# Value products of two key steps issued together, in an attention and LoRA-router kernel on one core

## The reference, cut to what matters

```python
# x: (2, 2048, 1024); wq, wo: (1024, 1024); wk, wv: (1024, 32); 32 heads of 32, one shared key/value head
h = layernorm(x)
q = (h @ wq).reshape(B, T, 32, 32); k = h @ wk; v = h @ wv
scores = einsum('bqhd,bkd->bhqk', q, k) / sqrt(32)      # causal
probs  = softmax(scores)
out    = einsum('bhqk,bkd->bqhd', probs, v) @ wo
x = x + layernorm(out)
h = layernorm(x)
router = 8 * softmax(h @ Wr.T + br)                      # 8 experts
low    = einsum('bsd,hrd->bshr', h, A)                   # rank 16 each
x = x + layernorm(2 * einsum('bshr,hor,bsh->bso', low, B, router))
```

## Time and profile before

| what | value |
|---|---|
| median of three runs | 3582.85 us |
| the profiled execution: its time, its span | 3581.36 us, 3579.6 us |
| TensorE busy | 3306.6 us, 92% |
| VectorE busy | 2299.5 us, 64% |
| GpSimd busy | 2121.2 us, 59% |
| ScalarE busy | 1567.7 us, 44% |
| mean granted TensorE clock | 0.966 |

### The profile page before, as it was taken

How to read it: one execution, slowest core, us unless ns; L and a number is a source line. 1 busy time by engine, 2 the same in 40 slices (tenths; PEclk the granted TensorE clock), 3 DMA queues, 4 the chain that set the end, 5 groups by cost and what they waited for, 6 DMA issues and landing times.

```text
span 3579.6 us, 45027 instructions
## 1 busy us (share of the span) xinstructions
PE 3306.6 (92%) x15784; PEld 1612.1 (45%) x15784; DVE 2299.5 (64%) x5996; ACT 1567.7 (44%) x3121; POOL 2121.2 (59%) x773
## 2 busy tenths in 40 slices
PE   5789998999999999999987999999999999999897
PEld 3344444444444444443444444444445444444333
DVE  3557776767777767764355667667777676666605
ACT  1233344444454545455422234444445454445552
POOL 0234666756756777876423256766666667776870
PEclk8899999999999999999998899999999999999998
DMA  3312111101110100101111121111111010000000
GB/s 84 122 49 71 41 48 36 54 28 42 34 36 16 60 22 28 33 22 31 60 48 48 36 66 42 48 37 53 28 39 36 22 30 28 27 27 24 31 1 24
DMA packets 132897, 144.00 MB, mean 40 GB/s; under 512 B 28088, under 2 KB 93624, under 8 KB 132672
## 3 DMA queue, kind: packets, MB, share of 16 engines
q1 hardware_dynamic: 132672, 141.13, 13.5%
HBM read 72.91 MB, written 16.78 MB: 25 GB/s over the span
## 4 chain that ended last, share of the span: by engine, by line
PE 57%; POOL 21%; DVE 10%; issue 5%; ACT 5%; SPq 2%; DMA 1%; POOLq 0%; ACTq 0%; DVEq 0%
POOL ds L597 15%; PE ps L1232 10%; PE ps L1250 10%; PE ps L1341 9%; PE ps L1220 8%; PE ps L1206 8%; DVE mx L869 4%; POOL ds L594 3%; ACT pr L672 2%; PE ps L1259 2%; PE ps L1281 2%; SPq L493 1%; POOL xr L614 1%; PE ps L1370 1%; PE ps L1382 1%
## 5 line engine op out<-in xcount | busy, mean ns | idle before, releaser
L672 ACT ACTIVATE pr<-ps 128x512 f32<-128x512 f32 (+3 forms) x2560 | 1304.6, 533 | 1546.9 <-PE ps L1232 1032.0
L597 POOL TENSOR_TENSOR ds<-ds,pr 128x2048 f32<-128x2048 f32 (+1 forms) x376 | 1518.7, 4039 | 207.1 <-ACT pr L672 179.0
L1232 PE MATMUL ps<-qs,ks 98*128 98x512 f32 (+3 forms) x2560 | 1366.8, 539 | 83.8 <-ACT pr L672 67.0
L869 DVE TENSOR_REDUCE mx<-ps 128x1 f32<-128x512 f32 x1536 | 996.8, 682 | 438.0 <-PE ps L1220 432.8
L1220 PE MATMUL ps<-ks,qs 96*128 96x512 f32 (+3 forms) x2560 | 969.8, 389 | 53.9 <-DMA qs<-q 27.1
L1232 PEld LDWEIGHTS ps<-qs,ks 98*128 98x128 f32 x2560 | 490.7, 192 | 776.7 <-ACT pr L672 497.8
L866 DVE CUSTOM_DVE_ANT_0 ps<-ps,mask_qk 128x128 f32<-128x128 f32 (+3 forms) x1024 | 492.0, 497 | 447.2 <-PE ps L1220 443.2
L1220 PEld LDWEIGHTS ps<-ks,qs 96*128 96x128 f32 x2560 | 498.9, 197 | 287.1 <-issue 135.5
L1250 PE MATMUL ps<-pr,vs 128*32 128x512 f32 (+3 forms) x5120 | 616.6, 554 | 7.0 <-POOL pr L604 6.8
L1206 PE MATMUL ps<-xT,wq_sb 128*128 128x512 f32 x1024 | 525.6, 614 | 13.7 <-DVE ks L930 10.3
L1341 PE MATMUL ps<-wo_sb,ao 128*128 128x512 f32 x896 | 461.5, 613 | 24.1 <-DVE q L858 24.1
(11 more groups left out here) (147 smaller groups left out, 1967.8 us busy)
## 6 DMA issues: line engine op xcount, KB each, us to landing
qs<-q SPq DMA_DIRECT2D x768, 64.0 KB, 2.0
wq_sb<-in_L_attn_wq_dram SPq DMA_DIRECT2D x64, 512.0 KB, 4.3
t<-in_L_attn_x_dram SPq DMA_DIRECT2D x32, 512.0 KB, 6.7
xr<-in_L_attn_x_dram SPq DMA_DIRECT2D x28, 512.0 KB, 3.6
out_dram<-xr SPq DMA_DIRECT2D x28, 512.0 KB, 2.6
qs<-mT SPq DMA_DIRECT2D x256, 4.0 KB
wo_sb<-in_L_attn_wo_dram SPq DMA_DIRECT2D x1, 4096.0 KB, 14.0
xT<-in_L_attn_x_dram SPq DMA_DIRECT2D x4, 512.0 KB, 5.1
```

The source lines that it names most:

```text
L597: nc.gpsimd.tensor_tensor(ds[:, :, c0:], ds[:, :, c0:], this, ALU.add).then_inc(added, 1)
L672: nc.scalar.activation(pr[:, k % NS, g, c0:], ps[:, PST + head(n, t, g) % NPS, c0:], ACT.Exp, scale=SCALE).then_inc(exp_done, 1)
L869: nc.vector.tensor_reduce(found, seen, AX.X, ALU.max).then_inc(mx_done, 1)
L1232: last = nc.tensor.matmul(ps[:, bank, c0:], ks[0:STK + 2, c:c + P], qs[0:STK + 2, n % NS, g, c0:], start=True, stop=not by_mask)
```

## The change

The values of two steps are issued together in every even step t: those of steps t-2 and t-1, behind the second score, or behind the third where one of the two is a masked diagonal step. In step 0 they are those of the unit before's last two steps. Odd steps hold none, but for the last step of the last unit, which holds those of the step before, as it did. ScalarE's copy of the finished values moves from slot 2 to slot 3 of the next unit.

```diff
+    def value_steps(n, t):
+
+        if n == UN - 1 and t == steps(n) - 1:
+            return [(n, t - 1)]
+        if t % 2:
+            return []
+        n_, t_ = (n, t) if t else (n - 1, steps(n - 1))
+        return [(n_, t_ - 2), (n_, t_ - 1)] if n_ >= 0 else []
...
-            put(2, "ACT", "pv", n - 1)
+            put(3, "ACT", "pv", n - 1)
...
-                    n_, t_ = (n, t - 1) if t else (n - 1, steps(n - 1) - 1)
-                    if n_ >= 0 and g == (2 if zeroed(n_, t_) else 1):
-                        values(n_, t_)
+                    for n_, t_ in value_steps(n, t):
+                        if g == (2 if any(zeroed(*x) for x in value_steps(n, t)) else 1):
+                            values(n_, t_)
```

## The result

The changed kernel takes 3644.82 us (median of five runs, 3643.41 to 3650.34), the kernel before 3583.64 us on the same chip (3578.75 to 3590.13). The ratio is 1.0171, with a 95% interval of 1.0158 to 1.0185: 61 us slower, where 42 faster were forecast. The profiled execution has a span of 3648.5 us, 68.9 more than the 3579.6 of before.

What follows compares the result with a forecast made beforehand. TensorE's own stream, busy 92% of 3579.6 us, was taken as the bound. 61 us from merging, less 8 for uneven steps and 12 for VectorE, gave 41 us less: 3541 us, with 8 in 10 for 3500 to 3580.

Steps and rivals of the forecast that it cites:

- What bounds the kernel: Whole kernel: TensorE's stream sets most of the time, 57% of the chain; GpSimd's additions some, 21%.
- (1) the merge: Value groups on TensorE: 319 merges save 0.33 us each, 58% of it on the chain, 61 us less.
- the 0.34: TensorE at value groups: a change from full width to strips and back costs 1.20 - 0.86 = 0.34 us.
- (2) Values and their waits: TensorE's waits for exponentials and mask at the values, 7.0 us: gain of 0 to 7 us, taken as 0.
- (3) The copy: ScalarE's copy of finished values, one slot later: 0, within 64 x 0.1 us either way.
- (4) Uneven steps: Odd steps without other work: 41 bare pairs gain nothing instead of 0.33 us each, 8 us less gain.
- The clock, dismissed in the rivals: TensorE in leaner odd steps: half clock from idle gaps, set aside as granted clock was 1.00; no chance of its own.
- (5) VectorE: VectorE gets no new tile of maxima's scores during a pair's 2.06 us; 12 us lost, bounds 0 and 137.
- The slower rival, "by the block": Even steps: last two exponentials come 0.86 us later, delaying GpSimd's additions and later exponentials; 3631 us, chance 0.08.

Runs made afterwards that it cites:

- experiment 1: Against the kernel before: values held back only in the 106 odd steps with other TensorE work behind the second score; 3560.71 us, ratio 0.993.

## Why the prediction was wrong

- **What bounds the kernel, and (1) the merge.** Right in kind and nearly in size. A second group costs 0.85 us. Floors fell by 83 us over all of TensorE's stream, 0.26 a merge, against 105 at 0.33 each; I have no count of where the other 22 are. One reading behind the 0.34 doesn't hold: in the earlier trace rows the score at 1640.91, with a wait and no values ahead of it, is followed after 0.34 us too (1641.25), so 1642.95 to 1643.29 shows nothing of the exit from the strips. The readings from the chain stand without it. Where it can work undisturbed it pays: 106 merges give 24 us, 0.23 each, against the 0.58 x 0.33 = 0.19 of the forecast.
- **(2) Values and their waits.** Right: the matmuls' idle time ahead of the values fell from 7.0 to 1.3 us, in the page's group for L1259.
- **(3) The copy.** Right, 0.9992.
- **(4) Uneven steps. The step that failed.** I costed the odd steps from bare pairs at the exponentials' pace and counted only the 41 pairs with nothing at all in both steps, 8 us. What counts is the place behind the second score, and it is empty in 214 of 320 odd steps. The values there worked while the next exponential was finished. The distance from a score for the maxima to the next score grew by 66 us, 46 of them at these places, and in the 19 units at full clock in both kernels 108 merges gained 2.8 us where 0.19 each would be 21. The term was 8 us; by these units, which are those that kept the clock and no random choice, it is nearly as large as the gain.
- **The clock, dismissed in the rivals. The step that cost most.** I read a granted clock of 1.00 in four units that have values in every step, and concluded for a kernel that has none in every second one. The rows cited were of the state that the change removes. The changed kernel has 136 us more at half clock. At 0.32 us each that is an estimate of 44 us, from the spread between executions; the ceiling is 68; a line through the 64 units and the start, change in time against change in half-clock time, has a slope of 0.47 and gives 65 of the 69 us. So the clock's part is some 44 to 68 us, most or all of the loss, where the forecast had nothing.
- The rule of the Trainium skill that I set aside (TensorE: Matmul & The Clock Gate, Why this matters for your kernels) asks for no long idle gaps between bursts. Here leaner steps did bring the clock down, as it warns, but with no long gap: TensorE was 83% busy in the 6.5 us before a fall, and its longest gap was 0.68 us.
- **(5) VectorE.** Not shown. Weight loads of the maxima's scores waited 30 us more, of which an unknown part is hidden, against the 12 of the forecast. No run separates it.
- **The slower rival, "by the block".** The right sign, but not its mechanism. GpSimd's additions do wait more for exponentials (210.0 against 179.0 us), and GpSimd's part of the chain grew. But if the block itself cost, the 106 merges of experiment 1 would cost too, and they gain.

Left open: why the same program falls to half clock in unit 22 and not in unit 54; and how the 61 us divide between waits and clock exactly, as time at half clock contains waits, and slower stretches may be both cause and effect of a low clock.

## What to carry to other kernels

A group of instructions that can be moved may be the cover of a wait at its old place. Ask of every place that a change empties what TensorE does there next, and for whom it waits, before counting what is gained where the group arrives. Merge where other work stands at the old place (here 106 of 320), and leave the rest. And read the granted clock of a place as it will be after the change: a stretch of lean steps can cost as much by the clock as the merge saved, or more.

## What the runs showed of the hardware

- The clock fell without a long pause: after 6.5 us with TensorE busy 83% and no gap over 0.68 us, it was 0.51 over the next 6.8 us. Work of 1.85 us then took 3.64.
- 858 score products more in 214 lean steps cost 13 us in one kernel and 84 us in another; time at half clock fell from 379 to 234 us in the first and from 243 to between 190 and 250 in the second. Added work was nearly free where it brought the clock back and filled waits.
- Over 78 executions of twelve kernels, 1 us more at half clock goes with 0.32 us more time within a kernel. Between the kernel before and the changed one, 30 units with 163 us more at half clock take 78 us more.
- Going from full-width products to 32-column strips and back costs 0.34 us; a second strip group right behind the first costs 0.85 us into the same bank, 0.86 into another.
